# Perceiver block: the first batch's keys stacked by two queues, the first four pairs ahead of the query stores' completion, and five value steps between the two sets of key steps

## The chip, the cores and the metric

The kernel runs on one core of a Trainium2 chip. Its time is the device time of one execution in microseconds (us), as the median of several runs. The profile is that of one more execution; the profiled execution has its own time, given beside its span below. TensorE is called PE, VectorE DVE, ScalarE ACT, GpSimd POOL, and SyncE, which here only issues transfers, SP.

## The reference, cut to what matters

Three layers follow each other on a latent array x of 32 batches x 64 queries x 256 channels: a cross attention over a context of 1601 keys a batch, a feed-forward layer on a closed-form circuit, and a mixture of experts. The change lies in the cross attention, and only in its first batch:

```
x = x + xattn(layernorm(x), ctx, ctx)
q = split_heads(query @ Wq.T + bq)          # 16 heads of 16 channels
k = split_heads(key @ Wk.T + bk)            # key = value = ctx, 32 x 1601 x 256
v = split_heads(value @ Wv.T + bv)
score = einsum('bhqd,bhkd->bhqk', q, k) * SCALE
attn = softmax(score)
out = einsum('bhqk,bhkd->bhqd', attn, v)
return out @ Wp.T + bp
```

## The kernel before, in words

**Numbers in two parts.** Operands of the projections are split into a high part (fp32r) and a low part, and a product is made of three matmuls (`three`: high x high, low x high, high x low). Keys are split likewise: after a key step, DVE writes `k_hi` and then `k_lo` from the PSUM bank (L377, L379).

**Steps.** One batch's keys and values are made in 15 steps. A key step ("k", m, q) fills 402 key columns of channel half m (m = 0 or 1, q = 0 to 3) with six matmuls of 402 columns. A value step ("v", t) fills two tiles of 128 keys with twelve matmuls of 256 columns; ("v", 12) is the rest of 65 keys alone, six matmuls. Value steps come in the order 0, 2, 4, 12, 6, 8, 10. In the first batch the steps have an order of their own, `FIRST_ORDER`: four key steps of half 0, three value steps, four key steps of half 1, the other four value steps. PE makes them in that order into five PSUM banks in turn, and waits before step s for the copy of step s - 4 (`kv_copied`); DVE copies them out in the same order (`copy_step`). All other batches are made one ahead, between the score matmuls of the batch before.

**Stacking.** The score matmuls of a pair of heads contract over 96 partitions: high keys, low keys and high keys again, 32 partitions each. `stack_keys` makes this stack `k_st` (tile a_kst) by transfers from `k_hi` and `k_lo`: for each half m and each piece z (two pieces of 804 columns) 4 pairs x 3 transfers of 32 x 804, so 12 transfers of 100.5 KB for (m, z) and 48 for a batch. They go from SP's queue. The semaphore `stacked[m][z]` counts them. `k_hi` and `k_lo` hold only one half m at a time: before DVE writes the first columns of a piece of half 1, it waits for all 12 transfers of the same piece of half 0 (L377 in `copy_step`).

**Memory.** `k_st` lies over the buffers of the query projection, which are no longer used after it: pairs 0 to 3 over the normalised rows `x_sb` and part of their transpose `xT`, pairs 4 to 7 over the rest of `xT` and over `q_hi` and `q_lo`, the split queries. These go to HBM in four groups (`store_queries`, two transfers of 512 KB each), counted by `stored`; the tile a_bd, the other operand of the scores, is filled from there.

**Around the change.** SP issues the stores of groups 2 and 3, waits until the stores of groups 1, 2 and 3 have landed (L194, L195), stacks (0,0), (0,1) and (1,0), and then enters its loop, which begins with (1,1), six fills of a_bd for batch 1 and the load of a later batch's context. PE starts the scores of pair 0 once all 15 steps are copied and both pieces of half 0 are stacked; DVE takes each pair's scores out of PSUM with a running minimum (L359), ACT makes the exponentials (L290), and PE turns the result (L575). ACT's own queue issues no transfer.

Of the kernel before, what the change touches and what calls it, by code (L numbers as in the profile page):

```python
# [6 lines left out]
F32 = mybir.dt.float32  # L7
# [9 lines left out]
NC = D // P  # L17
PAIRS = H // 2
QK = 4
KQ = 402  # L20
SKP = QK * KQ
# [9 lines left out]
K_ORDER = [("k", i // QK, i % QK) for i in range(KSTEPS)]  # L31
HALF_STEP = 3
V_ORDER = [("v", t) for t in (*range(0, 2 * HALF_STEP, 2), KT - 1, *range(2 * HALF_STEP, KT - 1, 2))]

FIRST_ORDER = K_ORDER[:QK] + V_ORDER[:QK - 1] + K_ORDER[QK:] + V_ORDER[QK - 1:]
STEP_ORDER = [K_ORDER[0]] + [s for i in range(VSTEPS) for s in (V_ORDER[i], K_ORDER[i + 1])]

SLOT_STEPS = ((0,), (1, 2), (3, 4), (5, 6, 7), (8,), (9, 10), (11, 12), (13, 14))
# [1 line left out]
HALF = PAIRS // NC  # L40
STACK = 3 * 32
PIECES = 2
# [30 lines left out]
def cross_attention(nc, ctxT, x, q_scr, wq, bq, wk, bk, wv, bv, wp, rows, ident, x1_scr, x1_mv):  # L73
    with ExitStack() as ctx:
# [12 lines left out]
        k_st = sb("a_kst", [STACK, PAIRS, SKP], F32R)  # L87
# [53 lines left out]
        def _(sp):  # L141
# [5 lines left out]
                        src = q_scr[part, :, bass.ds(n * SQ, SQ)].rearrange("(p e d) t -> e d p t", e=2, d=HD)[e]  # L147
                        sp.dma_start(bd[r:r + HD, slot, :, SQ * e:SQ * (e + 1)].bitcast(F32), src).then_inc(q_loaded, 16)

            def stack_keys(n, m, z):  # L150

                sp.wait_ge(kv_copied, STEPS * n + order_of(n).index(("k", m, QK // PIECES * (z + 1) - 1)) + 1)
                cols = slice(z * SKP // PIECES, (z + 1) * SKP // PIECES)
                for j in range(HALF):
                    if z == 0 and j > 1 and not (isinstance(n, int) and n == 0):

                        sp.wait_ge(s_filled, PAIRS * (n - 1) + HALF * m + j + 1)
                    for i, part in enumerate((k_hi, k_lo, k_hi)):
                        sp.dma_start(k_st[32 * i:32 * i + 32, HALF * m + j, cols].bitcast(F32),
                                     part[32 * j:32 * j + 32, cols].bitcast(F32)).then_inc(stacked[m][z], 16)  # L160
# [30 lines left out]
            store_queries(2)  # L191
            store_queries(3)

            sp.wait_ge(stored[1], 32)  # L194
            sp.wait_ge(stored[2], 32 * 2)  # L195
            for m, z in ((0, 0), (0, 1), (1, 0)):
                stack_keys(0, m, z)

            def body(it, first, last):
                for b in range(2):  # L200
                    n = 2 * it + b
                    ahead = not (last and b == 1)
                    stack_keys(n, 1, 1)
                    if ahead:
                        if not (first and b == 0):

                            sp.wait_ge(s_filled, PAIRS * n)
                        fill_queries(n + 1, 1 - b)
                    if not last:
                        if not (first and b == 0):  # L210

                            sp.wait_ge(ctx_split, NC * (n + 1))
                        load_ctx(n + 2, 0)
                    if b == 0 and not first:

                        sp.wait_ge(x1_free, 16 * it - 15)
                        sp.dma_start(x_t[:], x[bass.ds(it - 1, 1)].rearrange("a p d -> (a p) d")).then_inc(x_loaded, 16)
                    if ahead:
                        stack_keys(n + 1, 0, 0)
                    if not last:  # L220

                        sp.wait_ge(ctx_split, NC * (n + 1) + 1)
                        load_ctx(n + 2, 1)
                    if ahead:
                        stack_keys(n + 1, 0, 1)
                    if b == 0 and not first:

                        sp.wait_ge(x1_summed, 2 * it)
                        sp.dma_start(x1_scr[bass.ds(it - 1, 1)].rearrange("a p d -> (a p) d"), x_t[:]).then_inc(x1_free, 16)
                    if ahead:  # L230
                        stack_keys(n + 1, 1, 0)
# [47 lines left out]
        @block.scalar  # L279
        def _(act):  # L280
            def copy_tiles(g, p, i):

                act.wait_ge(t_filled, TG * g + i + 1)
                nc.scalar.copy(pT[:, p % HALF, 4 * i:4 * i + 4, :], ps_t[:, i % 2, :].rearrange("p (t q) -> p t q", q=P)).then_inc(t_copied_act, 1)  # L284

            def exponentials(g, b, p):

                act.wait_ge(max_ready, g + 1)
                pr = probs[:, p % 2, 0:SK]
                nc.scalar.activation(pr, pr, ACT.Exp, bias=nmax[:, b, p:p + 1], scale=-1.0,  # L290
                                     accum_out=esum[:, b, p:p + 1]).then_inc(probs_ready, 1)

            def copy_rows(g):

                for k in range(NC):
                    i = NC * g + k
                    act.wait_ge(q_rows_filled, i + 1)
                    nc.scalar.copy(xT[:, k, tokens(g)], row_bank(i)).then_inc(q_rows_copied, 1)

            def high(g):  # L300

                act.wait_ge(wq_loaded, 48)
                if g > 1:

                    act.wait_ge(stored[g - 2], 32)
                for m in range(NC):
                    i = NC * g + m
                    act.wait_ge(q_filled, i + 1)
                    nc.scalar.activation(q_hi[:, g % 2, m, :], ps_s[:, i % 4, :], ACT.Identity, bias=bq_sb[:, m:m + 1]).then_inc(q_hi_done, 1)

            def first_high(k):
                act.wait_ge(first_loaded, 16)
                nc.scalar.copy(c_hi[:, 0, k, :], first_ctx[:, 0, k, :]).then_inc(ctx0_hi_done, 1)

            act.wait_ge(bd_zeroed, 1)
            nc.scalar.activation(esum[:, 0, 0:1], expo[:, 0:1], ACT.Exp)
            copy_rows(0)
            act.wait_ge(w_loaded, 32)
            nc.scalar.copy(w_hi[:], w_raw).then_inc(w_hi_done, 1)
            copy_rows(1)  # L320
            high(0)
            copy_rows(2)
            first_high(0)
            high(1)
            copy_rows(3)
            first_high(1)
            high(2)
            high(3)

            def body(it, first):  # L330
                for b in range(2):
                    n = 2 * it + b
                    for p in range(PAIRS):
                        g = PAIRS * n + p
                        prev = not first or b > 0 or p > 0
                        if prev:
                            copy_tiles(g - 1, (p - 1) % PAIRS, 0)
                            copy_tiles(g - 1, (p - 1) % PAIRS, 1)
                            if p % HALF == 0:
                                copy_tiles(g - 1, (p - 1) % PAIRS, 2)  # L340
                        exponentials(g, b, p)
                        if prev and p % HALF > 0:
                            copy_tiles(g - 1, (p - 1) % PAIRS, 2)

            for it in range(NT):
                body(it, it == 0)
            g = PAIRS * B - 1
            for i in range(3):
                copy_tiles(g, PAIRS - 1, i)
# [1341 lines left out]
```

## Time and profile before

| | |
|---|---|
| time, median of 3 runs | 2011.12 us (2010.55 to 2012.7) |
| profiled execution | 2009.8 us, its span 2008.0 us |
| PE busy | 1912.1 us (95%) |
| DVE busy | 1474.4 us (73%) |
| ACT busy | 1142.3 us (57%) |
| POOL busy | 613.6 us (31%) |
| DMA engines, q1 | 55.8% of the span |
| stages: query projection and first batch's steps | 0 to 64 us |
| cross attention | 64 to about 1440 us |
| circuit layer and experts | the rest |

The profile has one line for an instruction or a run of equal ones: start, duration, engine, line of the kernel, operation, tile written and tile read, and in brackets how long the engine was idle before it and what ended that. "SPq" rows are the issuing of transfers on SP. PEclk is the clock that TensorE was granted, 1.00 for 2.4 GHz and 0.50 for 1.2 GHz; a value between is a stretch with both. The DMA share is the mean busy share of the core's 16 DMA engines.

### The profile page before, as it was taken

The page shows a single profiled execution, that of the slowest core. Times are in us where ns is not written, and L with a number is a line of the kernel's source. Part 1 is how long each engine was busy: PE and PEld are TensorE (multiplying, and loading weights), DVE is VectorE, ACT ScalarE, POOL GpSimd, SP SyncE. Part 2 cuts the span into 40 slices and gives each one's busy share as a digit, 9 for nine tenths or more (in the row PEclk, how much of TensorE's full clock was granted, in tenths as well). Part 3 has the DMA queues.
Part 4 walks back from the last instruction along what each step waited for, and adds up shares of the span by engine and source line. Part 5 has one row for each costly group of instructions (what it writes and reads, how often), then busy time and mean ns, then how long its engine had stood idle before and what let it go on. Part 6 is the DMA issues. An engine that isn't in the chain of part 4 may idle for free. (4 is left out here: it accounts for less than half of the span.)

```text
span 2008.0 us, 46641 instructions
## 1 busy us (share of the span) xinstructions
PE 1912.1 (95%) x18834; PEld 1791.7 (89%) x18834; DVE 1474.4 (73%) x2801; ACT 1142.3 (57%) x1924; POOL 613.6 (31%) x616
## 2 busy tenths in 40 slices
PE   6899999999999999999999999999469799999998
PEld 4899999999999999999999999998347789999998
DVE  5677777787877877787787777877486656666656
ACT  2466666666666665666666665666475435555552
POOL 3222233222232222233222232320111216777750
PEclk9899999999999999999999999999879799999999
DMA  7666666666666666667666666665211425666633
GB/s 243 170 161 161 163 160 180 156 158 157 171 162 167 162 156 159 164 163 180 152 159 156 172 159 169 164 153 128 99 40 64 158 112 192 217 200 214 216 103 121
DMA packets 152615, 318.26 MB, mean 158 GB/s; under 512 B 58016, under 2 KB 83488, under 8 KB 148944
## 3 DMA queue, kind: packets, MB, share of 16 engines
q1 hardware_dynamic: 148176, 303.73, 55.8%
q0 software_dynamic: 4224, 11.54, 2.0%
q8 instruction: 150, 2.46, 0.5%
q14 instruction: 65, 0.53, 0.1%
HBM read 136.49 MB, written 20.58 MB: 78 GB/s over the span
## 5 line engine op out<-in xcount | busy, mean ns | idle before, releaser
L284 ACT COPY a_pT<-a_pst 128x512 f32<-128x512 f32 x768 | 421.5, 583 | 412.9 <-PE a_pst L575 412.9
L290 ACT ACTIVATE a_probs<-a_probs,a_nmax 128x1601 f32<-128x1601 f32 x256 | 418.8, 1636 | 147.4 <-DVE a_probs L359 147.0
L359 DVE TENSOR_SCALAR_CACHE_REDUCE a_probs<-a_pss 128x1608 f32<-128x1608 f32 x256 | 467.3, 1825 | 13.5 <-PE a_pss L564 13.3
L575 PE MATMUL a_pst<-a_id,a_probs 128*128 128x128 f32 (+1 forms) x3328 | 450.0, 273 | 12.9 <-ACT a_pT L284 10.0
L575 PEld LDWEIGHTS a_pst<-a_id,a_probs 128*128 128x128 f32 (+1 forms) x3328 | 380.6, 140 | 50.7 <-issue 21.9
L245 POOL TENSOR_TENSOR a_tick<-a_tick 128x1 f32<-128x1 f32 x62 | 12.0, 194 | 959.0 <-DMA a_raw<-in_ctxT 926.6
L377 DVE TENSOR_SCALAR a_khi<-a_psk,a_bk 128x402 fp32r<-128x402 f32 x250 | 158.5, 634 | 143.2 <-PE a_psk L529 141.5
L250 POOL TENSOR_TENSOR a_clo<-a_raw,a_chi 128x402 fp32r<-128x402 f32 x240 | 247.2, 1063 | 4.8
L527 PE MATMUL a_pso<-a_whi,a_chi 128*128 128x256 f32 (+1 forms) x806 | 241.2, 299 | 0.0
L564 PE MATMUL a_pss<-a_kst,a_bd 96*128 96x402 f32 x1024 | 239.0, 355 | 1.6 <-DVE a_probs L359 0.8
L529 PE MATMUL a_pso<-a_whi,a_clo 128*128 128x256 f32 (+1 forms) x806 | 226.6, 281 | 0.0
L528 PE MATMUL a_pso<-a_wlo,a_chi 128*128 128x256 f32 (+1 forms) x806 | 226.3, 281 | 0.0
L564 PEld LDWEIGHTS a_pss<-a_kst,a_bd 96*128 96x128 f32 x1024 | 182.9, 189 | 15.2 <-issue 12.5
L595 PE MATMUL a_pso<-a_pT,a_v 128*32 128x128 f32 x6656 | 195.9, 274 | 0.2
L527 PE MATMUL a_psk<-a_chi,a_whi 128*128 128x402 f32 x500 | 193.7, 387 | 0.0
L1516 PE MATMUL e_psg<-e_xh,e_guh 128*128 128x256 f32 x660 | 190.2, 288 | 1.9 <-DVE e_xl L1247 1.5
L595 PEld LDWEIGHTS a_pso<-a_pT,a_v 128*32 128x32 f32 x6656 | 178.2, 110 | 13.0 <-issue 13.0
L1518 PE MATMUL e_psg<-e_xh,e_gul 128*128 128x256 f32 x660 | 187.5, 284 | 0.0
L1517 PE MATMUL e_psg<-e_xl,e_guh 128*128 128x256 f32 x660 | 187.4, 284 | 0.0
L528 PE MATMUL a_psk<-a_clo,a_whi 128*128 128x402 f32 x500 | 172.9, 346 | 0.0
L529 PE MATMUL a_psk<-a_chi,a_wlo 128*128 128x402 f32 x500 | 172.7, 345 | 0.0
L379 DVE SCALAR_TENSOR_TENSOR a_klo<-a_psk,a_bk,a_khi 128x402 fp32r<-128x402 f32 x250 | 159.0, 636 | 8.9
(239 smaller groups left out, 3519.6 us busy)
## 6 DMA issues: line engine op xcount, KB each, us to landing
a_kst<-a_khi SPq DMA_DIRECT2D x1024, 100.5 KB, 2.5
a_kst<-a_klo SPq DMA_DIRECT2D x512, 100.5 KB, 2.5
a_raw<-in_ctxT SPq DMA_DIRECT2D x60, 804.0 KB, 5.7
e_gur<-in_wgu SPq DMA_DIRECT2D x24, 1408.0 KB, 9.1
e_dr<-in_wd SPq DMA_DIRECT2D x24, 768.0 KB, 9.7
a_bd<-q_scr SPq DMA_DIRECT2D x192, 32.0 KB, 1.9
e_big<-ys_scr SPq DMA_DIRECT2D x8, 512.0 KB, 7.4
a_pT<-in_ctxT SPq DMA_DIRECT2D x2, 1608.0 KB, 9.0
```

Of the source, the lines that this page charges most:

```text
L250: last = nc.gpsimd.tensor_tensor(out=c_lo[:, s, k, cols], in0=src[:, cols], in1=c_hi[:, s, k, cols].bitcast(F32), op=ALU.subtract)
L284: nc.scalar.copy(pT[:, p % HALF, 4 * i:4 * i + 4, :], ps_t[:, i % 2, :].rearrange("p (t q) -> p t q", q=P)).then_inc(t_copied_act, 1)
L290: nc.scalar.activation(pr, pr, ACT.Exp, bias=nmax[:, b, p:p + 1], scale=-1.0, accum_out=esum[:, b, p:p + 1]).then_inc(probs_ready, 1)
L359: nc.vector.tensor_scalar(probs[:, p % 2, :].rearrange("p (b k) -> p b k", b=QK), ps_s[:, :, 0:KQ], -SCALE, None, ALU.mult, ALU.min, accum ...
L527: nc.tensor.matmul(out, a[0], b[0], start=start, stop=False)
L528: nc.tensor.matmul(out, a[0], b[1], start=False, stop=False)
L529: return nc.tensor.matmul(out, a[1], b[0], start=False, stop=stop)
L564: mm = nc.tensor.matmul(ps_s[:, q, 0:KQ], bd[:, b, p, :], k_st[:, p, q * KQ:(q + 1) * KQ], start=True, stop=True)
L575: mm = nc.tensor.transpose(ps_t[0:r, i % 2, (t % 4) * P:(t % 4 + 1) * P], probs[:, p % 2, t * P:t * P + r], id_sb[:])
L595: mm = nc.tensor.matmul(ps_o[32 * j:32 * j + 32, 0:P], v_sb[0:r, b, t, 32 * p:32 * p + 32], pT[0:r, j, t, :], start=(t == 0), stop=(t == K ...
L1516: nc.tensor.matmul(out, a[0], b[0], start=start, stop=False)
L1518: return nc.tensor.matmul(out, a[1], b[0], start=False, stop=stop)
```

## The change

Three edits, all of the first batch:

1. **Order.** `FIRST_ORDER` has five value steps between the two sets of key steps, instead of three, and two behind them, instead of four.
2. **Two queues.** Of the four pairs of each (m, z), SP stacks pairs 0 and 2, and ACT stacks pairs 1 and 3 with a function of its own, `stack_first_keys`. ACT issues its 24 transfers after its last work on the queries and before its first exponential. (1,1) is stacked ahead of SP's loop instead of at its start.
3. **The wait.** The wait for the stored queries stands ahead of (1,0), on both queues, instead of ahead of (0,0).

```diff
-FIRST_ORDER = K_ORDER[:QK] + V_ORDER[:QK - 1] + K_ORDER[QK:] + V_ORDER[QK - 1:]
+FIRST_ORDER = K_ORDER[:QK] + V_ORDER[:QK + 1] + K_ORDER[QK:] + V_ORDER[QK + 1:]
...
-            def stack_keys(n, m, z):
+            def stack_keys(n, m, z, of=range(HALF)):
...
-                for j in range(HALF):
+                for j in of:
...
-            sp.wait_ge(stored[1], 32)
-            sp.wait_ge(stored[2], 32 * 2)
-            for m, z in ((0, 0), (0, 1), (1, 0)):
-                stack_keys(0, m, z)
+            for m in range(NC):
+                for z in range(PIECES):
+                    if (m, z) == (1, 0):
+
+                        sp.wait_ge(stored[1], 32)
+                        sp.wait_ge(stored[2], 32 * 2)
+                    stack_keys(0, m, z, range(0, HALF, 2))
...
-                    stack_keys(n, 1, 1)
+                    if not (first and b == 0):
+                        stack_keys(n, 1, 1)
...
+            def stack_first_keys(m, z):
+
+                act.wait_ge(kv_copied, FIRST_ORDER.index(("k", m, QK // PIECES * (z + 1) - 1)) + 1)
+                cols = slice(z * SKP // PIECES, (z + 1) * SKP // PIECES)
+                for j in range(1, HALF, 2):
+                    for i, part in enumerate((k_hi, k_lo, k_hi)):
+                        act.dma_start(k_st[32 * i:32 * i + 32, HALF * m + j, cols].bitcast(F32),
+                                      part[32 * j:32 * j + 32, cols].bitcast(F32)).then_inc(stacked[m][z], 16)
...
             high(2)
             high(3)
+            stack_first_keys(0, 0)
+            stack_first_keys(0, 1)
+            for g in (1, 2):
+
+                act.wait_ge(stored[g], 32 * g)
+            stack_first_keys(1, 0)
+            stack_first_keys(1, 1)
```

**On SP's queue**, before, behind the stores of the last queries (q_scr is their scratch in HBM; a_kvc is `kv_copied`, q_stored1 and q_stored2 are `stored`):

```order
L172 DMA q_scr<-q_hi 128x2x512 [waits q_qs]
L172 DMA q_scr<-q_lo 128x2x512
L159 DMA a_kst<-a_khi 32x804 [waits a_kvc,q_stored2,q_stored1]
L159 DMA a_kst<-a_klo 32x804
L159 DMA a_kst<-a_khi 32x804 x2
L159 DMA a_kst<-a_klo 32x804
```

and in the changed kernel at the same place:

```order
L172 DMA q_scr<-q_hi 128x2x512 [waits q_qs]
L172 DMA q_scr<-q_lo 128x2x512
L159 DMA a_kst<-a_khi 32x804 [waits a_kvc]
L159 DMA a_kst<-a_klo 32x804
L159 DMA a_kst<-a_khi 32x804 x2
L159 DMA a_kst<-a_klo 32x804
L159 DMA a_kst<-a_khi 32x804
L159 DMA a_kst<-a_khi 32x804 [waits a_kvc]
L159 DMA a_kst<-a_klo 32x804
L159 DMA a_kst<-a_khi 32x804 x2
L159 DMA a_kst<-a_klo 32x804
L159 DMA a_kst<-a_khi 32x804
```

The wait for the stores is gone from the first stacking transfer, and a piece is six transfers on this queue instead of twelve.

**On ACT**, in the changed kernel, between the last two rows of the query projection (q_hi) and the first exponential; before, the exponential L290 stood right behind the q_hi rows. Two of the four pieces are shown with what follows the last:

```order
L313 ACTIVATE q_hi<-a_pss,q_bq 128x512 [waits q_qf]
L325 DMA a_kst<-a_khi 32x804 [waits a_kvc]
L325 DMA a_kst<-a_klo 32x804
L325 DMA a_kst<-a_khi 32x804 x2
L325 DMA a_kst<-a_klo 32x804
L325 DMA a_kst<-a_khi 32x804
...
L325 DMA a_kst<-a_khi 32x804 [waits a_kvc]
L325 DMA a_kst<-a_klo 32x804
L325 DMA a_kst<-a_khi 32x804 x2
L325 DMA a_kst<-a_klo 32x804
L325 DMA a_kst<-a_khi 32x804
L294 ACTIVATE a_probs,a_esum<-a_probs,a_nmax 128x1601 [waits a_mr]
```

All 24 transfers of ACT stand ahead of its first exponential.

**On DVE**, before, from the last copy of half 0's keys (a_klo) to the first scores (a_probs, L359); a_v is the tile of the values:

```order
L379 SCALAR_TENSOR_TENSOR a_klo<-a_pss,a_bk,a_khi 128x402
L384 COPY a_v<-a_pss 128x512
L384 COPY a_v<-a_psk 128x512
L384 COPY a_v<-a_pss 128x512
L377 TENSOR_SCALAR a_khi<-a_pss,a_bk 128x402
...
L379 SCALAR_TENSOR_TENSOR a_klo<-a_psk,a_bk,a_khi 128x402
L386 COPY a_v<-a_pss 65x256
L384 COPY a_v<-a_pss 128x512 x3
L359 TENSOR_SCALAR a_probs,a_nmax<-a_pss 128x1608
```

and in the changed kernel:

```order
L399 SCALAR_TENSOR_TENSOR a_klo<-a_pss,a_bk,a_khi 128x402
L404 COPY a_v<-a_pss 128x512
L404 COPY a_v<-a_psk 128x512
L404 COPY a_v<-a_pss 128x512
L406 COPY a_v<-a_pss 65x256
L404 COPY a_v<-a_pss 128x512
L397 TENSOR_SCALAR a_khi<-a_pss,a_bk 128x402
...
L399 SCALAR_TENSOR_TENSOR a_klo<-a_pss,a_bk,a_khi 128x402
L404 COPY a_v<-a_pss 128x512 x2
L379 TENSOR_SCALAR a_probs,a_nmax<-a_pss 128x1608
```

The value copies of 65 keys and of one double tile have moved ahead of half 1's first key copy; two double tiles are left behind its last.

## Rows read from the trace of the kernel before

**Rows 1.** Stretches of the run: window, length, busy per engine, PEclk, DMA share, GB/s

```profile
50.00:52.00 2.00, 0.00 (x0) 0.00 (x0) 0.82 (x2) 0.00 (x0) 0.00 (x0) 0.51 0.67 154
65.00:75.00 10.00, 8.42 (x60) 7.70 (x59) 7.78 (x11) 5.97 (x9) 0.00 (x0) 1.00 0.62 144
130.00:230.00 100.00, 99.85 (x1108) 95.28 (x1097) 77.44 (x139) 60.91 (x94) 28.91 (x30) 1.00 0.67 169
```

**Rows 2.** DVE in order of time, from half 0's keys to the first scores

```profile
36.72 0.63 DVE L379 SCALAR_TENSOR_TENSOR a_klo<-a_pss,a_bk,a_khi 128x402 fp32r<-128x402 f32 x1
...
40.30 0.68 DVE L384 COPY a_v<-a_psk 128x512 f32<-128x512 f32 x1
40.90 0.68 DVE L384 COPY a_v<-a_pss 128x512 f32<-128x512 f32 x1
51.15 0.64 DVE L377 TENSOR_SCALAR a_khi<-a_pss,a_bk 128x402 fp32r<-128x402 f32 x1 [9.57 <-DMA a_kst<-a_khi]
...
58.77 0.64 DVE L377 TENSOR_SCALAR a_khi<-a_pss,a_bk 128x402 fp32r<-128x402 f32 x1 [5.11 <-DMA a_kst<-a_khi]
...
61.21 0.41 DVE L386 COPY a_v<-a_pss 65x256 f32<-65x256 f32 x1
...
62.99 0.69 DVE L384 COPY a_v<-a_pss 128x512 f32<-128x512 f32 x1 [0.18 <-PE a_pss L529]
64.78 1.83 DVE L359 TENSOR_SCALAR_CACHE_REDUCE a_probs<-a_pss 128x1608 f32<-128x1608 f32 x1 [1.10 <-PE a_pss L564]
```

**Rows 3.** SP's issuing of transfers in order of time

```profile
35.35 1.34 SPq L172 DMA_DIRECT2D q_scr<-q_lo  x1
41.86 0.63 SPq L159 DMA_DIRECT2D a_kst<-a_khi  x1
...
48.89 1.23 SPq L159 DMA_DIRECT2D a_kst<-a_khi  x2
...
56.52 1.23 SPq L159 DMA_DIRECT2D a_kst<-a_khi  x2
...
72.97 0.59 SPq L159 DMA_DIRECT2D a_kst<-a_khi  x1
```

**Rows 4.** SP's waits from 25 to 130 us: total, times, longest

```profile
SPq L152 <- DMA q_scr<-q_lo: 5.1, 1, 5.1
```

**Rows 5.** DMA engines in short stretches, columns as in Rows 1

```profile
38.00:39.00 1.00, 1.00 (x10) 1.00 (x10) 1.00 (x2) 0.00 (x0) 1.00 (x2) 1.00 1.00 383
...
40.00:41.00 1.00, 1.00 (x9) 1.00 (x8) 1.00 (x3) 0.00 (x0) 1.00 (x2) 1.00 0.06 25
...
43.00:44.00 1.00, 1.00 (x7) 1.00 (x6) 0.00 (x0) 0.00 (x0) 0.00 (x0) 1.00 0.70 164
46.00:48.00 2.00, 0.00 (x0) 0.00 (x0) 0.00 (x0) 0.00 (x0) 0.00 (x0) 1.00 0.67 159
...
80.00:82.00 2.00, 2.00 (x16) 1.99 (x15) 1.26 (x4) 1.59 (x2) 0.00 (x0) 1.00 0.99 286
```

**Rows 6.** PE in order of time, from half 0's keys to the first scores

```profile
36.03 0.28 PE L527 MATMUL a_pss<-a_whi,a_chi 128*128 128x256 f32 x1
...
40.35 0.35 PE L527 MATMUL a_pss<-a_chi,a_whi 128*128 128x402 f32 x1
...
41.45 0.34 PE L527 MATMUL a_pss<-a_chi,a_whi 128*128 128x402 f32 x1
...
45.33 0.28 PE L529 MATMUL a_pss<-a_whi,a_clo 128*65 128x256 f32 x1
...
53.10 0.41 PE L529 MATMUL a_pss<-a_whi,a_clo 128*128 128x256 f32 x1
53.31 0.41 PE L527 MATMUL a_pss<-a_whi,a_chi 128*128 128x256 f32 x1
...
63.74 1.01 PE L564 MATMUL a_pss<-a_kst,a_bd 96*128 96x402 f32 x4 [0.78 <-DVE a_v L384]
```

**Rows 7.** ACT's first exponential, from the order of time

```profile
66.66 1.63 ACT L290 ACTIVATE a_probs<-a_probs,a_nmax 128x1601 f32<-128x1601 f32 x1 [32.67 <-DVE a_probs L359]
```

## The prediction

> **What bounds the kernel now.** I read the stretches first, since the change touches only the first batch. Over most of the attention TensorE works 99.85 of 100 us [rows 1]: nothing else bounds it there, so whatever the start gains is kept, and whatever moves in other queues is hidden as long as TensorE is not made to wait. Between 65 and 75 us it already works 8.42 of 10 us. The time that can be had lies before the first scores, which start at 63.74 [rows 6].
>
> The order of time on DVE shows what holds that start. Four key steps of half 0 are copied, three value copies end near 41.5, and then DVE stands 9.57 us for the first stacked piece and, two key steps later, 5.11 us for the second [rows 2]. The four value copies behind the last key step end at 62.99 + 0.61 = 63.6, and the scores follow 0.14 us later. So the chain is: piece (0,0) landed (51.15), piece (0,1) landed (58.77), two key copies, four value copies, scores.
>
> SP's queue shows why the pieces are late. The keys of the first piece are copied at 36.72 + 0.64 = 37.36 [rows 2], but the first stacking transfer is issued at 41.86, after 5.1 us of waiting for the query stores [rows 3, 4]. From there SP issues without a break, 0.637 us apart (23 transfers from 41.86 to 56.52) [rows 3]; the twelfth leaves within the row of 48.89, and its piece is there at 51.15, 1.65 us after its issue ends at 49.50. The DMA engines meanwhile are 0.67 to 0.70 busy at 159 to 164 GB/s [rows 5]: they are not full, the issuing sets the pace.
>
> **The change part by part.** Durations come from the profiled execution, 2009.8 us with a span of 2008.0; its median over runs is 2011.12, so I work out a saving and take it from the median.
>
> *The wait moved behind (0,0) and (0,1).* The first issue moves from 41.86 to 37.36, 4.5 us. It does not all reach the landing: the stores are still on the engines, share 1.00 at 383 GB/s, until close to 40, and then a trickle of 25 GB/s, about what one of 16 engines moves, runs to about 41.8 [rows 5]. Before, data flowed from about 43, 1.1 us after the issue; now it could flow from 38.5, beside 1.2 us of store traffic on 15 engines and 3.3 us on the last one. I keep both ends. Ahead of (1,0) the wait costs nothing: (1,0) cannot start until its keys are copied, near 49, long after the stores.
>
> *Two queues.* Each issues 6 of the 12 transfers of a piece. By issuing alone that is 6 x 0.637 = 3.8 us instead of 7.6. But one transfer keeps the engines busy for about 0.69 x 0.637 = 0.44 us, and the highest share the trace shows with stacking in it is 0.99 [rows 5], so a piece needs at least 12 x 0.44 = 5.3 us of the engines. The engines become the bound. A landing takes 0.5 us beyond the last data (1.65 less the 1.1 from issue to data). So piece (0,0) lands between 38.5 + 1.2 + 5.3 + 0.5 = 45.5 and 38.5 + 3.3 + 5.3 + 0.5 = 47.6, and piece (0,1) 5.3 us later, between 50.8 and 52.9. Without a reason to prefer one end I take the middle, 46.6 and 51.9; before it was 51.15 and 58.77.
>
> On two queues the Trainium skill speaks against a gain. "DMA: Bandwidth & Descriptors", section "Issuing engines are not separate DMA queues", says that transfers issued by several engines run on the same 16 DMA engines, and that only the issuing time is saved, which is usually small beside the transfer. Here the issuing is the larger part by the trace, 0.637 us against 0.44, so by rule and rows together the saving per transfer is the difference and no more; taken as "small, nothing is saved" it would give the first rival below.
>
> *Five value steps between.* A value step takes TensorE (40.35 - 36.03) / 3 = 1.44 us, that of 65 keys about half, a key step 1.10 [rows 6]. Half 1's first key step is then filled at 40.35 + 0.72 + 1.44 + 1.10 = 43.6 instead of 41.45, before the piece is there (46.6), so this costs nothing; if the piece came at 43, it would be the bound. The eleventh step onward: k 44.7, 45.8, 46.9, value 48.3, and the last value step, which needs the copy of half 1's first keys (47.8), about 49.8. Behind the last key copy DVE has only two value copies, both filled, 0.60 us each by the rows at 40.30 and 40.90: 1.2 us. Before, the tail ran from 61.21 to 63.6, 2.4 us, its last copy waiting for a TensorE at half clock [rows 2, 6]. This part saves 1.2 us.
>
> *The sum to the first scores.* Piece (0,1) at 51.9, two key copies 2.44 (58.77 to 61.21), value copies 1.2, 0.14 to the scores: 55.7 instead of 63.74, 8.0 us earlier.
>
> *The clock.* TensorE's granted clock falls to 0.51 in the idle stretch at 50 to 52, after work that ended at 45.6 [rows 1, 6]. In the changed kernel TensorE is idle from about 49.8 to 55.7, so I expect the first scores at 1.2 GHz; before they ran at full clock, four matmuls in 1.01 us. At half clock 256 columns take 0.21 us from start to start [rows 6], so 402 columns 0.33 instead of about 0.18: 0.6 us for the first pair, up to 0.6 more for the second. The key step between lies beside DVE's 1.83 us. I take 1.0, with ends 0 and 1.5.
>
> *ACT.* It has no work from its last query row to 66.66 [rows 7], so its first 18 transfers are free. The last six come after the last key copy, at 54.3, and end at 54.3 + 3.8 = 58.1 by SP's pace; the first exponential is due at 55.7 + 2.92 + 0.6 = 59.2. Covered with 1.1 us to spare. The trace shows no transfer issued by ACT; the nearest rows are SP's, 0.63 for a stacking transfer and 1.34 for the store behind a full queue [rows 3]. I take 0.64 to 0.88 (twice 0.44, if ACT is held to the engines' pace); at 0.88 its 24 transfers end at 37.4 + 21.1 = 58.5, still in time.
>
> *SP after it.* (1,1) ends at about 58.1 instead of 73.6, so the fills of a_bd and the next context come some 15 us earlier, ahead of all that needs them. (1,0) is issued from 49.0 and lands, behind (0,1), near 57.2; DVE wants it for batch 1's first keys at 55.7 + 1.04 + 1.83 + 0.6 = 59.2. Hidden, by 2 us.
>
> Saving: 8.0 - 1.0 = 7.0 us. Forecast 2011.12 - 7.0 = 2004.1 us. By the ends of the terms (landing of (0,1) 1.05 either way, clock 0.5 to 1.0) it runs from 2002 to 2005.7; allowing some 10% for how well the engines fill, 2001.5 to 2007.
>
> **The rivals.** *The engines take no more than before.* Stacking alone runs at 159 to 164 GB/s throughout [rows 5], perhaps because small transfers leave gaps that a second queue does not fill. Then a piece still takes 7.6 us: (0,0) lands near 48.9, (0,1) near 56.5, scores at 60.3, saving 3.4 less 1.0: 2008.7. If ACT's issuing is held back with it, to 1.27 us each, its 24 transfers end at 37.4 + 30.5 = 67.9, 1.2 later than the first exponential before: 2012.4. For it: that constant rate. Against: the share of 0.99 at 286 GB/s when a context load lies beside stacking, while SP's issuing did not slow. About 2010.
>
> *The queues do not disturb each other at all.* Piece (0,0) is issued by 41.2 and lands with the stores, about 43.9, (0,1) at 45.0 + 1.65 = 46.7; then half 1's steps and the last value step on TensorE (49.8) are the bound, copied at 50.5, scores at 50.6: 13.1 us earlier, no fall of the clock: 1998. It needs the engines to move 320 GB/s of stacking, twice what they show. Against it stands their share of 0.7.
>
> *ACT becomes the wall, and the kernel is slower.* One mechanism: ACT issues all 24 transfers ahead of its first exponential, each held up. The first exponential was at 66.66, so it decides from (66.66 - 37.4) / 24 = 1.22 us for one. At the 1.34 us of SP's widest row [rows 3] ACT is done at 69.6, 2.9 us late: 2014. For it: that row, behind a full queue, the state in which ACT starts here. Against: 23 rows at 0.637.
>
> **How the numbers follow.** Forecast 60%, engines take no more 20%, undisturbed queues 13%, ACT the wall 7%. A measurement of this kernel can tell about 0.2% (4.0 us) from no change. Faster by more than that is below 2007.1: the forecast nearly whole, the undisturbed queues, a little of the first rival: 0.73. Within 0.2%, 2007.1 to 2015.1: the first rival and part of the third, 0.23. Slower 0.04. The range of 8 in 10 leaves out half of the undisturbed queues and the dear half of the two others: 1999.5 to 2010.3.
>
> **What would show it.** Right: SP and ACT both issue a_kst from 37.4; DVE's two waits end near 46.6 and 51.9 and the DMA share lies at 0.9 or more between; the first scores start near 55.7 with PEclk at 0.5; ACT's last issue ends ahead of its first exponential; from 75 us on TensorE is as full as before, and everything stands 7 us earlier. Wrong: a share that stays at 0.7 with pieces 7.6 us apart (first rival), scores before 52 (second), an exponential that waits for nothing but its own queue (third), or any new wait of TensorE in the stretch after 75 us, which no part of this sum holds.

## The result, and the profile after

The changed kernel takes 2002.95 us (median of 14 runs) against 2012.23 us for the kernel before on the same chips: ratio 0.9961, 95% interval 0.9952 to 0.9970, so 7.8 us faster (6 to 10); the two medians alone differ by 9.3 us, inside that interval. The forecast was a saving of 7.0 us, 2004.1 us in a range of 1999.5 to 2010.3. The profiled execution took 2004.61 us, its span 2002.8 us.

| marks in the profiled execution, us | before | after | earlier by |
|---|---|---|---|
| first stacking transfer issued | 41.86 | 36.96 | 4.9 |
| DVE's wait for (0,0) / (0,1) ends | 51.15 / 58.77 | 46.21 / 51.43 | 4.9 / 7.3 |
| first pair's scores | 63.74 | 55.20 | 8.5 |
| second pair's scores | 66.68 | 58.84 | 7.8 |
| third pair's scores | 72.43 | 64.61 | 7.8 |
| last scores of the attention | 1424.44 | 1416.45 | 8.0 |
| end of the span | 2008.0 | 2002.8 | 5.2 |

DVE in order of time in the changed kernel, from half 0's keys to the first scores, which answers to [rows 2]:

```profile
36.30 0.64 DVE L399 SCALAR_TENSOR_TENSOR a_klo<-a_pss,a_bk,a_khi 128x402 fp32r<-128x402 f32 x1
...
46.21 0.64 DVE L397 TENSOR_SCALAR a_khi<-a_pss,a_bk 128x402 fp32r<-128x402 f32 x1 [3.06 <-DMA a_kst<-a_khi]
...
51.43 0.64 DVE L397 TENSOR_SCALAR a_khi<-a_pss,a_bk 128x402 fp32r<-128x402 f32 x1 [2.69 <-DMA a_kst<-a_khi]
...
53.87 1.28 DVE L404 COPY a_v<-a_pss 128x512 f32<-128x512 f32 x2
56.95 1.83 DVE L379 TENSOR_SCALAR_CACHE_REDUCE a_probs<-a_pss 128x1608 f32<-128x1608 f32 x1 [1.80 <-PE a_pss L584]
```

The two waits are still there, 3.06 and 2.69 us instead of 9.57 and 5.11. The pieces land 5.22 us apart instead of 7.62.

The DMA engines in short stretches, columns as in [rows 1]; they answer to [rows 5]:

```profile
44.00:46.00 2.00, 2.00 (x13) 2.00 (x12) 0.00 (x0) 0.00 (x0) 0.00 (x0) 1.00 0.98 251
46.00:48.00 2.00, 2.00 (x17) 2.00 (x16) 1.75 (x3) 0.00 (x0) 0.00 (x0) 1.00 1.00 243
...
52.00:54.00 2.00, 0.00 (x0) 0.00 (x0) 1.93 (x5) 0.00 (x0) 0.00 (x0) 0.50 1.01 254
54.00:56.00 2.00, 0.80 (x2) 0.80 (x3) 1.15 (x2) 0.00 (x0) 0.00 (x0) 0.50 0.97 228
```

With two queues the engines are full or nearly so, where one queue kept them at 0.7 and 160 GB/s: the share is 0.97 to 1.01 in these rows, and 0.93 and 0.94 at 206 GB/s in the two stretches between them. The last two rows have PEclk at 0.50: the scores start cold. Cold means at 1.2 GHz here and below, warm means at 2.4 GHz.

TensorE in order of time, which answers to [rows 6]:

```profile
49.41 0.28 PE L549 MATMUL a_pss<-a_whi,a_clo 128*128 128x256 f32 x1
55.20 1.71 PE L584 MATMUL a_pss<-a_kst,a_bd 96*128 96x402 f32 x4 [5.52 <-DVE a_v L404]
...
58.84 1.02 PE L584 MATMUL a_pss<-a_kst,a_bd 96*128 96x402 f32 x4
...
64.61 0.91 PE L584 MATMUL a_pss<-a_kst,a_bd 96*128 96x402 f32 x4
```

and ACT's own queue and ACT, which answer to [rows 7]:

```profile
36.97 0.62 ACTq L325 DMA_DIRECT2D a_kst<-a_khi  x1
...
57.95 0.84 ACTq L325 DMA_DIRECT2D a_kst<-a_khi  x1
58.84 1.63 ACT L294 ACTIVATE a_probs<-a_probs,a_nmax 128x1601 f32<-128x1601 f32 x1 [25.26 <-DVE a_probs L379]
```

The first scores take 1.71 us instead of 1.01. ACT's 24 transfers end at 57.95 + 0.84 = 58.79; DVE's result for the first exponential is there at 56.95 + 1.83 = 58.78. The two meet to 0.01 us, and the exponential starts 0.05 us after them.

From the third pair on the two traces run alike, 8 us apart; stretches of the changed kernel, columns as before:

```profile
65.00:75.00 10.00, 9.96 (x76) 9.56 (x75) 8.19 (x13) 6.55 (x10) 5.74 (x6) 1.00 0.75 201
...
130.00:230.00 100.00, 99.83 (x1117) 95.12 (x1119) 79.51 (x143) 62.29 (x95) 24.90 (x26) 1.00 0.63 157
```

The span is only 5.2 us shorter, though the attention ends 8.0 earlier. That is scatter behind the change: from the last scores to the end of the span it took 583.6 us before and 586.4 after, and between 581.2 and 589.2 in the twelve experiments, whose code there is the same. So the experiments are judged by their marks in the first 75 us, and by ratios only where these are wide apart. From the third scores to the last ones the 14 traces take 1351.1 to 1353.2 us, so a difference of less than about 2 us at the last scores tells nothing either.

### The profile page after: what moved, and what is told of

It reads as the page before. It is cut to its first block and busy times, and to the rows that moved or that the text cites. A ratio compares the mean times of both kernels' runs of the same rounds, so it can differ in the third digit from the quotient of the medians.

```text
span 2002.8 us, 46642 instructions
## 1 busy us (share of the span) xinstructions
PE 1912.1 (95%) x18834; PEld 1792.3 (89%) x18834; DVE 1475.4 (74%) x2801; ACT 1142.3 (57%) x1924; POOL 613.8 (31%) x616
## 5 line engine op out<-in xcount | busy, mean ns | idle before, releaser
L249 POOL TENSOR_TENSOR a_tick<-a_tick 128x1 f32<-128x1 f32 x62 | 12.1, 195 | 951.8 <-DMA a_raw<-in_ctxT 917.6
```

## The experiments

Each was run with the kernel before beside it; its marks come from one profiled execution. "First to third" is the time from the first pair's scores to the third's; it is 8.69 in the kernel before and holds all that the clock, ACT and DVE cost after the start. How far a mark scatters can be read from kernels that are the same up to it: in changed, kept warm, ACT 18 transfers and the two rows below it, the wait for (0,0) ends at 46.21 to 46.59 and that for (0,1) at 50.78 to 51.54. First to third is steadier: 9.39 to 9.41 in the changed kernel, no queues, wait not moved and ACT 18 transfers, and 8.68 or 8.69 in before, order not changed and gaps filled.

| kernel | (0,0) / (0,1) | first scores | first to third | third scores | last scores | ratio to before (95%) |
|---|---|---|---|---|---|---|
| before | 51.15 / 58.77 | 63.74 | 8.69 | 72.43 | 1424.44 | 1 |
| changed | 46.21 / 51.43 | 55.20 | 9.41 | 64.61 | 1416.45 | 0.9961 (0.9952 to 0.9970) |
| order only | 51.15 / 58.77 | 62.55 | 11.41 | 73.96 | 1425.06 | 1.0008 (0.9997 to 1.0019) |
| no queues | 47.45 / 55.07 | 58.84 | 9.40 | 68.24 | 1419.33 | 0.9979 (0.9967 to 0.9991) |
| wait not moved | 50.09 / 55.26 | 59.03 | 9.39 | 68.42 | 1421.63 | 0.9987 (0.9977 to 0.9998) |
| order not changed | 46.18 / 51.29 | 55.98 | 8.68 | 64.66 | 1415.77 | 0.9964 (0.9952 to 0.9977) |
| kept warm | 46.23 / 51.32 | 55.09 | 11.60 | 66.69 | 1418.66 | 0.9962 (0.9948 to 0.9976) |
| three pairs on ACT | 47.54 / 53.25 | 57.01 | 13.68 | 70.69 | 1421.87 | 0.9981 (0.9971 to 0.9991) |
| ACT 18 transfers | 46.50 / 51.54 | 55.31 | 9.39 | 64.70 | 1416.10 | 0.9965 (0.9951 to 0.9978) |
| the same, warm | 46.59 / 51.44 | 55.22 | 10.20 | 65.42 | 1417.83 | 0.9961 (0.9946 to 0.9976) |
| the same, gaps filled | 46.58 / 50.78 | 54.55 | 8.69 | 63.24 | 1414.45 | 0.9947 (0.9932 to 0.9961) |
| own buffers | no wait | 51.94 | 10.36 | 62.30 | 1415.03 | 0.9931 (0.9917 to 0.9944) |
| own buffers, wait freed | no wait | 52.43 | 10.21 | 62.64 | 1413.84 | 0.9940 (0.9925 to 0.9955) |
| the same, warm | no wait | 51.43 | 8.56 | 59.99 | 1412.36 | 0.9947 (0.9933 to 0.9962) |

**Order only.** The kernel before with the one changed line:

```diff
-FIRST_ORDER = K_ORDER[:QK] + V_ORDER[:QK - 1] + K_ORDER[QK:] + V_ORDER[QK - 1:]
+FIRST_ORDER = K_ORDER[:QK] + V_ORDER[:QK + 1] + K_ORDER[QK:] + V_ORDER[QK + 1:]
```

> Only the order: five value steps between the sets of key steps; one queue, the wait ahead of (0,0). Theory (each edit is worth what it moves on DVE's chain, and the cold start of TensorE belongs to the order): DVE's two waits end as before, near 51.2 and 58.8; the tail shrinks from 2.4 to 1.2 us, so the first scores start near 62.5 instead of 63.7, but now cold (1.7 us for the four matmuls instead of 1.0, PEclk 0.5), and the second pair's scores start only 0.3 to 0.6 us earlier than 66.7. The time is the same within what can be told: ratio 0.9995 to 1.0. Rival (the order is worth its full 1.2 us and the clock costs nothing here): second scores near 65.5.

The first scores come 1.2 us earlier, as the copies say, but the third come 1.5 us later. TensorE in this kernel:

```profile
62.55 1.71 PE L564 MATMUL a_pss<-a_kst,a_bd 96*128 96x402 f32 x4 [7.11 <-DVE a_v L384]
...
66.19 1.71 PE L564 MATMUL a_pss<-a_kst,a_bd 96*128 96x402 f32 x4
...
73.96 0.91 PE L564 MATMUL a_pss<-a_kst,a_bd 96*128 96x402 f32 x4
```

Both the first and the second pair run cold. Before, the three late value steps had TensorE at work just ahead of the scores. Its clock had fallen there too, but it was back as the scores began, by these rows at about 63.7 us:

```profile
60.00:62.00 2.00, 1.86 (x9) 1.87 (x10) 1.96 (x5) 0.00 (x0) 0.00 (x0) 0.57 0.66 158
62.00:64.00 2.00, 1.22 (x6) 0.92 (x6) 1.51 (x3) 0.00 (x0) 0.00 (x0) 0.57 0.67 159
64.00:66.00 2.00, 1.86 (x10) 1.51 (x9) 1.22 (x1) 0.00 (x0) 0.00 (x0) 1.00 0.65 154
```

With the order alone, PEclk stays at 0.50 long after the scores have begun:

```profile
64.00:68.00 4.00, 3.95 (x12) 2.93 (x11) 3.18 (x5) 1.72 (x2) 0.00 (x0) 0.50 0.68 159
```

It is back only at about 72.4. Up to the second scores the theory's marks held (66.19, 0.5 us earlier than 66.68). It had no term for what came behind them: from the second scores to the third it takes 7.77 us instead of 5.75. So the low stretch costs 2.7 us here (11.41 less 8.69), 0.7 of it ahead of the second scores and 2.0 behind them. Why the clock came back so late in this kernel stays open.

**No queues.** The changed kernel, all transfers from SP:

```diff
-                    stack_keys(0, m, z, range(0, HALF, 2))
+                    stack_keys(0, m, z)
...
-            stack_first_keys(0, 0)
-            stack_first_keys(0, 1)
-            for g in (1, 2):
-
-                act.wait_ge(stored[g], 32 * g)
-            stack_first_keys(1, 0)
-            stack_first_keys(1, 1)
```

> The changed kernel with one queue: SP stacks all four pairs, the wait stands ahead of (1,0), five value steps between. Theory (a single queue paces itself at 0.637 us): DVE's waits end near 37.4 + 7.6 + 1.7 = 46.7 and 54.3, or up to 1.5 us later where the stores are still in the way; first scores near 58.1, cold, second scores near 61.7, 5 us ahead of before; ratio 0.9975. Rival (the queues were the whole gain, the stores hold the engines anyway): first wait near 49 and second near 56.7, second scores near 64, ratio 0.9987.

The pieces are 7.62 us apart again, one queue's pace. They land 0.8 us later than 46.7 and 54.3, inside the 1.5 us allowed for the stores; SP's first two issues take 1.12 and 1.11 us here, with the stores on the engines, where later single ones take 0.60. The third scores are 3.6 us later than in the changed kernel: that is what the second queue is worth.

**Wait not moved.** The changed kernel with both waits ahead of (0,0):

```diff
-                    if (m, z) == (1, 0):
+                    if (m, z) == (0, 0):
...
+            for g in (1, 2):
+
+                act.wait_ge(stored[g], 32 * g)
             stack_first_keys(0, 0)
             stack_first_keys(0, 1)
-            for g in (1, 2):
-
-                act.wait_ge(stored[g], 32 * g)
```

> The changed kernel with the wait for the stored queries back ahead of (0,0) on both queues. Theory (two queues make the engines the bound, 0.44 us a transfer, 5.3 us a piece): issues begin near 41.5, DVE's waits end near 48.8 and 54.1, first scores near 57.9, cold, second near 61.5; 5 us ahead of before, ratio 0.9975. Rival (two queues gain only where the stores leave gaps): pieces 6.5 us or more apart, second scores 63 or later.

The pieces are 5.17 us apart, now with no stores beside them, so this spacing is the engines' own. DMA engines in this kernel, without the stores:

```profile
44.00:48.00 4.00, 4.00 (x27) 4.00 (x25) 0.00 (x0) 0.00 (x0) 0.00 (x0) 1.00 0.97 226
```

The first piece comes 1.3 us later than expected: 50.09 is 8.16 us after the first issue at 41.93, where the prediction's terms without stores give 1.1 + 5.3 + 0.5 = 6.9. A likely reason, not tested, is that both queues go on with (0,1) before (0,0) has landed. From 43 to 50 us the engines moved 7 x 228 = 1596 KB, by my estimate 15 to 16 transfers (32 x 804 x 4 = 102,912 bytes each), so three or four of (0,1) were done before the twelfth of (0,0) counted as landed. The third scores come 3.8 us later than in the changed kernel. Taken away one at a time, the wait and the queue are each worth about half, and the halves add: 3.6 + 3.8 = 7.4 of 7.8.

**Order not changed.** The changed kernel with the old line:

```diff
-FIRST_ORDER = K_ORDER[:QK] + V_ORDER[:QK + 1] + K_ORDER[QK:] + V_ORDER[QK + 1:]
+FIRST_ORDER = K_ORDER[:QK] + V_ORDER[:QK - 1] + K_ORDER[QK:] + V_ORDER[QK - 1:]
```

> The changed kernel with three value steps between and four behind, as before; two queues and the early start stay. Theory (the order buys 1.2 us on DVE and pays 0.7 to 1.0 of it back as a cold start): DVE's waits end near 46.2 and 51.4 as in the changed kernel, the last value copy ends near 56.3, first scores near 56.4 but warm or nearly so, second scores at 59.0 to 59.4, so within 0.6 us of the changed kernel's 58.8; ratio to before 0.9962 to 0.9968. Rival (the order is worth 1.2 us or more): second scores at 60 or later.

TensorE in this kernel:

```profile
55.98 1.00 PE L584 MATMUL a_pss<-a_kst,a_bd 96*128 96x402 f32 x4 [1.65 <-DVE a_v L404]
58.92 1.00 PE L584 MATMUL a_pss<-a_kst,a_bd 96*128 96x402 f32 x4 [0.83 <-DVE a_probs L379]
60.68 1.09 PE L595 MATMUL a_pst<-a_id,a_probs 128*128 128x128 f32 x8 [0.76 <-ACT a_probs L294]
```

It starts 0.8 us later, warm, and is level at the third scores (64.66 against 64.61); at the last it is 0.7 us ahead, which is within the scatter. The change of order is worth nothing that these traces can tell. The clock fell here too, at 49, but under value steps for which nothing waited, and it was back at about 52.4.

**Kept warm.** The changed kernel with matmuls whose result is never read:

```diff
+            for _ in range(27):
+                nc.tensor.matmul(ps_o[:, 0:KQ], w_hi[:, 0, 0, 0:P], w_hi[:].rearrange("p w k d -> p (w k d)")[:, 0:KQ], start=True, stop=True)
             pe.wait_ge(kv_copied, STEPS)
```

> The changed kernel with 27 matmuls of 402 columns into an unused bank (their result is never read) behind the first batch's last step, so that TensorE is not idle between 49.6 us and the first scores. Theory (the cold start costs 0.7 us, since the second pair's scores wait for DVE and ran warm already): first scores still start near 55.2 but take 1.0 us instead of 1.7, second scores start near 58.1 instead of 58.8, third near 63.9 instead of 64.6; ratio to before lower by 0.0003 than the changed kernel's 0.9961. Rival (the fall of the clock is paid elsewhere, or hidden by DVE): third scores at 64.6 as before.

The first scores take 1.01 us and the second start at 58.04, as expected; the third come 2.1 us later, not 0.7 earlier. ACT in this kernel:

```profile
57.08 1.62 ACTq L325 DMA_DIRECT2D a_kst<-a_klo  x1
58.72 0.88 ACTq L325 DMA_DIRECT2D a_kst<-a_khi  x1
59.65 1.63 ACT L294 ACTIVATE a_probs<-a_probs,a_nmax 128x1601 f32<-128x1601 f32 x1 [26.18 <-DVE a_klo L399]
```

The exponential was due at 56.14 + 1.83 = 57.97 and starts 1.7 us late, when ACT's last transfer is issued. TensorE waits for it 2.4 us, and PEclk is 0.59 in the stretch of 60 to 64. Both the theory and its rival failed here. ACT has only a part of the price: against the changed kernel the exponential is 0.8 us later and the third scores 2.1; the other 1.3 us lie behind the exponential, where the clock was low.

**Three pairs on ACT.** The changed kernel, 36 transfers on ACT and 12 on SP:

```diff
-                    stack_keys(0, m, z, range(0, HALF, 2))
+                    stack_keys(0, m, z, range(0, 1))
...
-                for j in range(1, HALF, 2):
+                for j in range(1, HALF):
```

> The changed kernel with pairs 1, 2 and 3 stacked by ACT (36 transfers) and pair 0 by SP (12). Theory (the engines set the pace, 0.45 us a transfer, until one queue alone needs more than its own 0.637; ACT's last transfers are nearly the wall already, ending at 58.79 with the exponential due at 58.78): the pieces land within 0.7 us of the changed kernel's 46.2 and 51.4, but ACT's last nine follow the last key copy, so its issues end near 60.2 to 61, and the first exponential starts there, 1.4 to 2.2 us late; third scores at 66.0 to 66.8; ratio to before 0.9968 to 0.9974. Rival (ACT's issues have slack, or the queue paces nothing): third scores at 64.6 to 65.2.

ACT in this kernel:

```profile
62.80 0.51 ACTq L325 DMA_DIRECT2D a_kst<-a_khi  x1
63.36 1.63 ACT L294 ACTIVATE a_probs<-a_probs,a_nmax 128x1601 f32<-128x1601 f32 x1 [29.45 <-issue]
```

ACT is the wall, more so than expected: the exponential is 4.5 us later than in the changed kernel and the third scores 6.1; behind the exponential PEclk falls once more, 0.68 in 64 to 68. The pieces land 1.3 and 1.8 us later than in the changed kernel, outside the 0.7 expected. They are 5.71 us apart, 9 x 0.634: the longer queue's own pace.

**ACT 18 transfers**, then **the same, warm**, then **the same, gaps filled.** (1,1) goes to SP; then the 27 matmuls are added; then 4 more ahead of the second scores and 4 behind them:

```diff
-                    stack_keys(0, m, z, range(0, HALF, 2))
+                    stack_keys(0, m, z, range(HALF) if (m, z) == (1, 1) else range(0, HALF, 2))
...
-            stack_first_keys(1, 1)
```

```diff
+                            if g == 1:
+                                fill(4)
                             pe.wait_ge(max_ready, g)
                             scores(b, p)
+                            if g == 1:
+                                fill(4)
                             pe.wait_ge(probs_ready, g)
```

> The changed kernel with (1,1) stacked by SP alone, so that ACT issues 18 transfers and not 24. Theory (ACT's last issue and its first exponential only just did not meet, 58.79 and 58.78): ACT ends its issues near 53.5, everything up to the third scores as in the changed kernel, 64.6; ratio 0.996. Rival (ACT's issues cost it something on average): third scores earlier by 0.5 us or more, ratio lower.

> The same with the 27 matmuls that keep TensorE from idling. Theory (a cold start costs 0.7 us, and what took it back in the earlier kernel with these matmuls was ACT, whose issues ended at 59.6, after the exponential was due): with ACT free, the first exponential follows DVE at once near 58.0, second scores near 58.1, third near 63.9, 0.7 us before the kernel without the matmuls and 2.8 before the earlier one. Rival (the matmuls themselves disturb what follows): third scores at 65 or later again.

> The kernel with 18 transfers on ACT and 27 unused matmuls, with 4 more ahead of the second pair's scores and 4 behind them, in the two stretches where TensorE waits 0.8 us each for DVE and for ACT. Theory (without them the clock fell at 59.9, behind those two gaps, and the low stretch of 3.3 us lay under matmuls that nothing hides): PEclk stays 1.00 from 48 to 66, the first half of the turned tiles takes 1.1 us instead of 2.0, third scores near 63.9 instead of 65.4, the last scores of the attention near 1415.5 instead of 1417.8. Rival (the fall has nothing to do with the gaps, it comes some time after the long wait): it falls near 60 again, third scores at 65 or later.

With 18 transfers ACT is free from 53.6 on and nothing changes (64.70 against 64.61): ACT is no cost in the changed kernel, only without reserve. The second pair runs cold here too (1.64 us instead of 1.02), at no cost to the third scores: the clock was back at about 60.4. Warm, the first exponential now follows DVE at once (58.14), yet the third scores are at 65.42. Stretches of this kernel:

```profile
56.00:57.00 1.00, 1.00 (x8) 0.99 (x6) 0.74 (x1) 0.00 (x0) 0.00 (x0) 1.00 0.86 255
57.00:58.00 1.00, 0.33 (x2) 0.00 (x0) 1.00 (x1) 0.00 (x0) 0.00 (x0) 1.00 0.59 138
58.00:59.00 1.00, 0.84 (x4) 0.67 (x4) 0.96 (x4) 0.86 (x1) 0.00 (x0) 1.00 0.04 10
59.00:60.00 1.00, 0.24 (x2) 0.09 (x2) 1.00 (x2) 0.86 (x2) 0.00 (x0) 0.89 0.84 195
60.00:61.00 1.00, 1.00 (x5) 1.00 (x6) 1.00 (x2) 0.00 (x0) 0.00 (x0) 0.50 0.62 148
```

The clock falls near 59.8, in the second of two gaps of 0.8 us, and the low stretch now lies under matmuls that nothing hides: 1.5 us, twice the cold start it replaced. With the two gaps filled as well, the stretches read

```profile
56.00:60.00 4.00, 3.91 (x23) 3.23 (x22) 3.96 (x5) 1.78 (x3) 0.00 (x0) 1.00 0.56 146
60.00:64.00 4.00, 4.00 (x32) 3.95 (x30) 1.85 (x5) 3.11 (x5) 0.00 (x0) 1.00 0.66 155
```

and first to third is 8.69 us, the value of the kernel before. (Its piece (0,1) also landed 0.7 us earlier, at 50.78, ahead of the eight added matmuls; of the 2.2 us at the third scores, 1.5 are the clock's.) That the two gaps by themselves bring the clock down is not shown, though. The kernel before has the same two, with PEclk at 1.00 from 64 to 72:

```profile
66.68 1.00 PE L564 MATMUL a_pss<-a_kst,a_bd 96*128 96x402 f32 x4 [0.82 <-DVE a_probs L359]
68.44 1.09 PE L575 MATMUL a_pst<-a_id,a_probs 128*128 128x128 f32 x8 [0.76 <-ACT a_probs L290]
```

So has order not changed (0.83 and 0.76 us), with PEclk at 1.00 from 56 to 68. Gaps filled was profiled once, and another moment of the fall in that one execution is a rival that no run excludes.

**Own buffers.** Half 1's keys of the first batch in two free stretches of a_pT, so that DVE needs no piece of half 0 to have landed:

```diff
+        own_hi, own_lo = (pT[:, i].rearrange("p t q -> p (t q)")[:, 0:SKP].bitcast(F32R) for i in (2, 3))
+        keys_of = lambda n, m: (own_hi, own_lo) if n == 0 and m == 1 else (k_hi, k_lo)
...
-                        if m == 1:
+                        if n == 0 and m == 1:
+                            dve.wait_ge(ctx_split, NC)
+                        elif m == 1:
...
+                        if g == 3:
+                            for piece in stacked[1]:
+                                act.wait_ge(piece, COPIES)
```

> The changed kernel with the first batch's keys of half 1 in two free stretches of the tile a_pT instead of k_hi and k_lo, so that DVE does not wait for the pieces of half 0; ACT stacks (0,0), (0,1) and (1,0), SP its half of these and all of (1,1). Theory (the chain is: landing of (0,1), then two key copies and two value copies, 3.8 us): DVE copies straight on and ends near 50.1, the first scores start at the landing of (0,1), near 51.5, with TensorE idle for only 2 us and so warm; second scores near 54.4, third near 60.2, 4.4 us ahead of the changed kernel; ratio to before near 0.994. Rival (the engines are the wall for what follows: (1,0) and (1,1) land no earlier, or ACT's 18 issues end too late): the first exponential or batch 1's first key copy waits for a_kst, and the third scores gain less than 3 us.

TensorE and DVE in this kernel:

```profile
51.94 0.97 PE L592 MATMUL a_pss<-a_kst,a_bd 96*128 96x402 f32 x4 [1.94 <-DMA a_kst<-a_khi]
```

```profile
57.18 0.64 DVE L405 TENSOR_SCALAR a_khi<-a_psk,a_bk 128x402 fp32r<-128x402 f32 x1 [2.38 <-DMA a_kst<-a_pT]
```

The scores start at the landing of (0,1), 3.3 us earlier, and 2.3 us of that are left at the third. The first pair runs warm, the second cold (1.71 us). The rival's wait is there: batch 1's first key copy waits for (1,0). That wait is the old guard of k_hi, which (1,0) no longer reads.

**Own buffers, wait freed**, and **the same, warm** with 11 unused matmuls:

```diff
-                        elif not (isinstance(n, int) and n == 0):
+                        elif n == 1:
+                            dve.wait_ge(stacked[0][z], COPIES)
+                        elif n > 1:
...
+                if g == 2:
+                    for piece in stacked[1]:
+                        dve.wait_ge(piece, COPIES)
```

> The previous kernel with half 1's keys in a_pT, with one wait moved: batch 1's first key copy no longer waits for the pieces of half 1 (they don't read k_hi and k_lo any more), the first write into a_pT behind them does. Theory (the 2.4 us that this copy waited at 57.18 held up the second pair's scores in PSUM and the clock fell in that gap): batch 1's first key copy starts right behind the first scores' copy, near 54.8; second scores still near 54.9; third scores near 60.6 if warm, 61.2 if cold, instead of 62.3; ratio to before 0.992 to 0.993, against 0.9931. Rival (the engines' backlog of stacking is the wall and the wait only moves): some other wait for a_kst before 70 us, third scores at 62 or later.

> The same, with 11 matmuls of 402 columns, whose result is never read, behind the first batch's last step. Theory (TensorE's clock falls after the idle stretch 49.6 to 51.9): PEclk stays 1.00 from 48 to 64, second scores take 1.0 us instead of 1.7, third scores near 60.5, 0.5 us or so before the kernel without them. Rival (the clock falls for the idle time after the first scores): no difference.

Freeing the wait alone brought nothing at the third scores (62.64, and 10.21 from first to third against 10.36). The time is in the rival's range, but its cause is not there: neither TensorE nor DVE nor ACT waits for a_kst between the first scores and 70 us. The second pair runs warm now, and the clock is low from about 58.0 to 61.4, under the matmuls that follow. With the 11 matmuls, TensorE shows PEclk 1.00 from 48 to 68, across gaps of 0.83 and 0.76 us, and

```profile
51.43 0.89 PE L597 MATMUL a_pss<-a_kst,a_bd 96*128 96x402 f32 x4
54.25 1.00 PE L597 MATMUL a_pss<-a_kst,a_bd 96*128 96x402 f32 x4 [0.83 <-DVE a_probs L385]
59.99 0.91 PE L597 MATMUL a_pss<-a_kst,a_bd 96*128 96x402 f32 x4
```

12.4 us ahead of before at the third scores and 12.1 at the last, 4.6 and 4.1 ahead of the changed kernel. By its marks this is the fastest version. Its ratio, 0.9947, doesn't part from the changed kernel's by the intervals; that of own buffers, 0.9931 (0.9917 to 0.9944), does. All three with own buffers beat the kernel before by their ratios, and the changed kernel by their marks at the third scores (2.0 to 4.6 us).

## Why the prediction was right, and where it was not

- **The wait moved.** Issues moved 4.9 us, not 4.5; 0.4 of it is that half 0's first keys were copied 0.4 us earlier in this execution, in code that did not change. The first piece landed at 46.21 (forecast 46.6, between the ends 45.5 and 47.6). Wait not moved puts its worth at 3.8 us. That the landing met the middle is luck: I took the middle without a reason, and two terms were off in opposite ways. Without the stores the first piece takes 8.16 us from issue to landing, not 6.9; with them it takes 46.21 - 36.97 = 9.24, so the stores cost 1.1 us, just under my low end of 1.2, and not the 2.2 of the middle.
- **Two queues.** The engines became the bound as worked out: pieces 5.22 us apart (forecast 5.3), the second at 51.43 (51.9), share 0.93 to 1.02 from 44 to 58 us. No queues gives 3.6 us for it. The rule that the prediction took from the Trainium skill ("DMA: Bandwidth & Descriptors", section "Issuing engines are not separate DMA queues"), that several issuing engines save only the issuing time, held here: the spacing fell from 0.637 us a transfer to 5.22 / 12 = 0.435, no further than the engines' own share. That this time is usually small beside the transfer did not fit this case: issuing was 0.637 us against 0.44.
- **Five value steps.** This step failed. I credited it 1.2 us and put the cold start into a term of its own, 1.0 us, as though it came with any version. The copies did shrink by 1.2 (53.87 to 55.1), but with the late value steps left in place (order not changed) TensorE was warm when the scores began: the cold start is the price of this very edit, and the two cancel (64.66 and 64.61). Alone, the edit costs 1.5 us at the third scores. The total came out near because both terms were in the sum.
- **The clock.** 0.72 us from first to third (9.41 less 8.69), forecast 1.0 with ends 0 and 1.5.
- **ACT.** The cover was claimed to be 1.1 us; there was none (58.79 against 58.78). Its issues took (58.79 - 36.97) / 24 = 0.91 us each, above the 0.64 to 0.88 I allowed, since both queues were held to the engines' pace (two transfers in 0.87 us) and slower still while the stores ran. The sum had a slip as well: it priced the last six, from 54.3 on, at SP's 0.637, and checked 0.88 only from 37.4 on. At 0.88 the last six end at 54.3 + 5.3 = 59.6, past the 59.2 at which the exponential was due, so no cover could be claimed at the dear end of the range. "ACT becomes the wall" had 7% and the kernel stands at its edge: in kept warm and three pairs on ACT the exponential did wait for the last issue, and was 0.8 and 4.5 us later than in the changed kernel; they lost 2.1 and 6.1 us at the third scores, the rest by the clock.
- **After 75 us.** TensorE is as full as before, 99.83 of 100 us against 99.85, and no new wait.
- **The size.** First scores 8.5 us earlier (forecast 8.0), third 7.8 (forecast 7.0), ratio 7.8. Of the difference of 0.8 at the third, 0.4 is the earlier front, 0.3 the clock, and 0.1 the rest. That the ratio gives the same 7.8 as the marks is partly chance, with an interval of 6 to 10.

Of the rivals, "the engines take no more than before" fell by the share, and "undisturbed queues" by the 5.2 us between pieces.

## What to carry to other kernels

When one queue issues many small transfers and the DMA share is well below 1, price the transfer twice, by the issuing (here 0.637 us) and by the engines' busy share of it (0.44): a second queue moves you from the first to the second and no further. Moving work away from just ahead of TensorE's next start can leave it to start cold; count the cold start against the edit that moves the work, and when you fill one idle stretch, look at PEclk in what follows too, since the low stretch may only move to a dearer place. Transfers issued by a computing engine stand in its order: their end belongs in the sum against that engine's next instruction.

## What was not expected of the hardware

- A low stretch of the clock costs by what lies under it. In the changed kernel it ran from about 51.8 to 58.6 us and cost 0.7; with 18 transfers on ACT it reached over the second pair too, to about 60.4, and cost the same; with the first stretch filled it ran from 59.8 to 63.2 and cost 1.5; in order only it lasted to 72.4 and cost 2.7.
- TensorE was idle only 1.9 us ahead of the first scores in both kernels with own buffers that were not kept warm, which then ran warm (0.97 us), and the clock still fell some microseconds later, at about 53.5 in one and 58.0 in the other. What decides the moment was not tried. Two kernels with added matmuls showed no fall up to 68 us, gaps filled and own buffers with 11 matmuls, each in one profiled execution. The second of them kept its clock across the same two gaps of 0.8 us in which it fell in the kernel with 18 transfers and 27 matmuls.
- The part of the program behind the attention takes 581 to 589 us from one execution to the next with the same code. That spread of 8 us is as large as the whole gain of the change, so marks inside the trace told apart what the total times could not.
